# Row tables laid out ahead of the first layer's loop, their padding rows cleared by ScalarE's queue in and behind that loop

## What is computed

```
h = jnp.maximum(_layernorm(x, axis=-1), 0.0)
x = x + _L0_gnn_ref(h, L0_gnn_W, L0_gnn_Bv, src, dst, edge_type_6)
h = jnp.maximum(_layernorm(x, axis=-1), 0.0)
x = x + _L1_gnn_ref(h, edge_attr_48, edge_attr_3, ...)      # edge_index = stack([src, dst])
...
    msg = jnp.concatenate([msg_s, msg_v.reshape(E, NV * 3)], axis=-1)
    out = _seg_mean(msg, src, N)          # first half of L1: mean over the edges of each src
...
    node1 = _seg_mean(msg, src, N)        # second half of L1
    return _bn_scalar(node1, bn1_gs, bn1_bs)
```

## Time and profile before

| | |
|---|---|
| median of 3 runs | 23958.75 us (23958.6 to 23959.51) |
| profiled execution, span from first to last instruction | 23994.0 us |
| a time of the profiled execution beside its span | none is given |
| VectorE, GpSimd, TensorE, ScalarE busy | 81%, 67%, 66%, 43% |
| all DMA queues | 1864.35 MB |

### The profile page before, as it was taken

How to read it: one execution, slowest core, us unless ns; L and a number is a source line. 1 busy time by engine, 2 the same in 40 slices (tenths; PEclk the granted TensorE clock), 3 DMA queues, 4 the chain that set the end, 5 groups by cost and what they waited for, 6 DMA issues and landing times.

```text
span 23994.0 us, 483073 instructions
## 1 busy us (share of the span) xinstructions
PE 15946.4 (66%) x137837; PEld 9487.0 (40%) x137837; DVE 19509.6 (81%) x37328; ACT 10304.8 (43%) x23410; POOL 15973.0 (67%) x18227
## 2 busy tenths in 40 slices
PE   5232777777777777766666577766777777777675
PEld 2221333333333333335656333333343333433333
DVE  8114888888888888889999888888888888888888
ACT  1001444444444444449999433333333333333332
POOL 0772777777777777777777566666666666666665
PEclk6555888888888888877777788888888888888887
DMA  4223333333333333324444222121222222222221
GB/s 142 52 50 132 111 111 106 110 111 111 106 109 111 111 107 109 111 97 118 118 118 118 65 40 40 40 40 40 40 40 40 40 40 40 40 40 40 40 40 37
DMA packets 1355296, 1864.35 MB, mean 78 GB/s; under 512 B 497379, under 2 KB 1137507, under 8 KB 1298789
## 3 DMA queue, kind: packets, MB, share of 16 engines
q1 hardware_dynamic: 835620, 1342.87, 18.2%
q0 software_dynamic: 483776, 469.85, 9.2%
q10 hardware_dynamic: 35842, 50.96, 0.6%
HBM read 1452.58 MB, written 409.77 MB: 78 GB/s over the span
## 4 chain that ended last, share of the span: by engine, by line
DVE 42%; issue 23%; POOL 16%; DVEq 6%; DMA 4%; ACT 3%; PE 3%; ACTq 1%; POOLq 1%; SPq 0%
POOL rows_d L731 13%; DVE arena L1767 11%; DVE arena L1716 7%; DVE arena L1774 6%; DVE arena L1758 5%; DMA rows_d<-arena 4%; DVEq L1794 4%; POOL arena L622 3%; DVE arena L1723 3%; ACT arena L1204 2%; DVE arena L1789 2%; DVE arena L1649 1%; DVE arena L1748 1%; DVE arena L1751 1%; PE wide L978 1%
## 5 line engine op out<-in xcount | busy, mean ns | idle before, releaser
L622 POOL DMA_INDIRECT arena<-s_tab,arena x7072 | 6703.2, 948 | 3772.1 <-issue 2032.1
L731 POOL DMA_INDIRECT rows_d<-arena x6656 | 6424.9, 965 | 2426.7 <-issue 2309.7
L1053 PE MATMUL wide<-w,arena 64*128 64x320 f32 x14144 | 3202.5, 546 | 2843.6 <-DVE arena L1758 2840.6
L978 PE MATMUL wide<-w,arena 64*128 64x320 f32 x13312 | 2975.3, 536 | 2257.1 <-DVE arena L1640 1639.7
L1649 DVE TENSOR_REDUCE arena<-arena 128x40 f32<-128x640 f32 x3328 | 2693.5, 809 | 428.3 <-DMA rows_d<-arena 427.6
L1640 DVE TENSOR_TENSOR arena<-wide,arena 128x640 f32<-128x640 f32 x3328 | 2653.0, 818 | 235.8 <-PE wide L978 167.0
L1053 PEld LDWEIGHTS wide<-w,arena 64*128 64x128 f32 x14144 | 1265.6, 210 | 3954.1 <-issue 2198.5
L1758 DVE TENSOR_TENSOR arena<-wide,arena 128x640 f32<-128x640 f32 x3536 | 2807.3, 815 | 0.2 <-PE wide L1053 0.2
L1767 DVE TENSOR_REDUCE arena<-arena 128x32 f32<-128x640 f32 x3536 | 2780.7, 806 | 0.0
L978 PEld LDWEIGHTS wide<-w,arena 64*128 64x128 f32 x13312 | 1189.1, 209 | 3150.7 <-issue 1778.3
L1039 PEld LDWEIGHTS duo<-ident_sb,arena 128*64 128x64 f32 x14144 | 1623.4, 175 | 1107.9 <-issue 1107.9
(11 more groups left out here) (208 smaller groups left out, 26899.6 us busy)
## 6 DMA issues: line engine op xcount, KB each, us to landing
arena<-rows_d SPq DMA_DIRECT2D x3536, 172.0 KB, 2.3
arena<-in_attr SPq DMA_DIRECT2D x208, 1024.0 KB
arena<-rel SPq DMA_DIRECT2D x208, 1024.0 KB
arena<-in_attr_rows SPq DMA_DIRECT2D x208, 768.0 KB
arena<-s_tab,arena POOLq DMA_INDIRECT x7072
rows_d<-arena POOLq DMA_INDIRECT x6656
rows_d<-zero ACTq DMA_DIRECT2D x198, 172.0 KB, 1.8
side<-arena SPq DMA_DIRECT2D x16, 1040.0 KB
```

Source lines behind the costliest of these rows:

```text
L622: pool.indirect_dma_start(out=dst_, out_offset=None, in_=tab, in_offset=bass.IndirectOffsetOnAxis(ap=idx, axis=0)).then_inc(signal, 16)
L731: pool.indirect_dma_start(out=rows_d[t // 4], out_offset=bass.IndirectOffsetOnAxis(ap=ui[:, s % GPT, t:t + 1], axis=0), in_=M[:, s % GPT, ...
L978: last = pe.matmul(wide[k % 2][:, j, 0:WN], hT[half, s % 2, k * P:(k + 1) * P], w2_sb[0][half, :], start=True, stop=True)
L1053: last = pe.matmul(wide[k % 2][:, j, 0:WN], bhT[half, s % 2, k * P:(k + 1) * P], w2_sb[1][half, :], start=True, stop=True)
```

## The change

The layout (stage 3) is moved ahead of the first layer's loop on VectorE, and its product ahead of that loop on TensorE. On ScalarE the stores of the bin numbers move ahead of the loop too, behind a wait for the layout (`laid_out`). The clears move into the loop: a turn copies out four groups, and behind each group's copy the two half groups of one bin are cleared, for `cleared` turns; later turns run without. The bins that are left and the two closing half groups are cleared behind the loop, and the square root comes behind those.

```diff
--- before.py
+++ after.py
@@ tensor
+            pe.wait_ge(spread_done, 1)
+            half = TPG * HB // 2
+            for i in range(2):
+                pe.matmul(wide[0][:, i, 0:half], ones[0:TPG * LO, :], spread[0:TPG * LO, i * half:(i + 1) * half],
+                          start=True, stop=True).then_inc(count_done, 1)
+
             pe.wait_ge(R.set_up, 1)
...
-            pe.wait_ge(spread_done, 1)
-            half = TPG * HB // 2
...
@@ scalar
             act.wait_ge(bound_out, 1)
-            turns = act.value_load(last_turn_sb[0:1, 0:1], min_val=2, max_val=TURNS - 1) + 1
+            last_turn = act.value_load(last_turn_sb[0:1, 0:1], min_val=2, max_val=TURNS - 1)
             R = R0
+            act.wait_ge(laid_out, 1)
+            act.dma_start(bin_d.rearrange("(h p j) -> p h j", h=2, j=8), gbin).then_inc(bin_out, 16)
+            act.wait_ge(bin_out, 16)
+            act.dma_start(bin_sb[:, :], bin_d.unsqueeze(0)).then_inc(bin_out, 16)
...
+            def clear_bin(b):
+                for h in range(2):
+                    clear_rows(h, act.value_load(zrow[0:1, h, bass.ds(b, 1)], min_val=0, max_val=DUMP * HALF))
+
+            clearing = act.alloc_register("clearing")
+            act.reg_mov(clearing, last_turn)
+            act.reg_alu(clearing, clearing, NB // GPT, ALU.min)
+            cleared = act.snap(clearing, min_val=2, max_val=NB // GPT)
...
                     last.then_inc(R.out_ready, 1)
+                    if clears:
+                        clear_bin(g)
...
             with act.Else():
-                with act.Fori(0, turns) as it:
-                    out_copies(it, False)
-            root(small[:, 1, :], 2, sqrt_out)
...
-            with act.Fori(0, NB) as b:
-                for h in range(2):
-                    clear_rows(h, act.value_load(zrow[0:1, h, bass.ds(b, 1)], min_val=0, max_val=DUMP * HALF))
+                with act.Fori(0, cleared) as it:
+                    out_copies(it, False, True)
+                with act.Fori(cleared, last_turn + 1) as it:
+                    out_copies(it, False, False)
+            with act.Fori(cleared * GPT, NB) as b:
+                clear_bin(b)
             for h in range(2):
                 clear_rows(h, act.value_load(zrow[0:1, h, HB:HB + 1], min_val=0, max_val=(NG + NB) * HALF))
+            root(small[:, 1, :], 2, sqrt_out)
...
@@ vector
             dve.sem_inc(R.x_free, GPT)
             dve.sem_inc(R.inputs_free, GPT)
-            turns = dve.value_load(last_turn_sb[0:1, 0:1], min_val=2, max_val=TURNS - 1) + 1
...
             dve.wait_ge(hot_used, PIECES)
             HT = TPG * LO
             link(tt(spread[0:HT, 0:HT], banks[3][0:HT, 0:HT], tmask[0:HT, :], ALU.mult))
...
             dve.sem_inc(laid_out, 1)
+            turns = dve.value_load(last_turn_sb[0:1, 0:1], min_val=2, max_val=TURNS - 1) + 1
...
```

More of the change, by code:

```diff
@@ L927, in _ @@
                     sum0_window(it)
-            pe.wait_ge(spread_done, 1)
-            half = TPG * HB // 2
-            for i in range(2):
-                pe.matmul(wide[0][:, i, 0:half], ones[0:TPG * LO, :], spread[0:TPG * LO, i * half:(i + 1) * half],
-                          start=True, stop=True).then_inc(count_done, 1)
             def edges():
@@ L1164, in out_copies @@
                     last.then_inc(R.out_ready, 1)
+                    if clears:
+                        clear_bin(g)
             act.wait_ge(R.set_up, 1)
             with act.If(act.value_load(any_wide[0:1, 0:1], min_val=0, max_val=1) > 0):
-                with act.Fori(0, turns) as it:
-                    out_copies(it, True)
+                with act.Fori(0, cleared) as it:
+                    out_copies(it, True, True)
+                with act.Fori(cleared, last_turn + 1) as it:
+                    out_copies(it, True, False)
             with act.Else():
-                with act.Fori(0, turns) as it:
-                    out_copies(it, False)
-            root(small[:, 1, :], 2, sqrt_out)
[L1175 to L1182, removed]
-            with act.Fori(0, NB) as b:
-                for h in range(2):
-                    clear_rows(h, act.value_load(zrow[0:1, h, bass.ds(b, 1)], min_val=0, max_val=DUMP * HALF))
+                with act.Fori(0, cleared) as it:
+                    out_copies(it, False, True)
+                with act.Fori(cleared, last_turn + 1) as it:
+                    out_copies(it, False, False)
+            with act.Fori(cleared * GPT, NB) as b:
+                clear_bin(b)
             for h in range(2):
                 clear_rows(h, act.value_load(zrow[0:1, h, HB:HB + 1], min_val=0, max_val=(NG + NB) * HALF))
+            root(small[:, 1, :], 2, sqrt_out)
             def edges():
@@ L1519, in _ @@
             dve.sem_inc(R.inputs_free, GPT)
+            dve.wait_ge(hot_used, PIECES)
+            HT = TPG * LO
+            link(tt(spread[0:HT, 0:HT], banks[3][0:HT, 0:HT], tmask[0:HT, :], ALU.mult))
+            link(red(gbin_f[0:HT, 0:LO], spread[0:HT, 0:HT].rearrange("p (t l) -> p l t", l=LO), AX, ALU.add))
+            link(tt(spread[0:HT, :].rearrange("p (w l) -> p w l", l=LO), ident_sb[0:HT, 0:HT].unsqueeze(2).broadcast_to([HT, HT, LO]),
+                    gbin_f[0:HT, 0:LO].unsqueeze(1).broadcast_to([HT, HT, LO]), ALU.mult))
@@ new lines, in _ @@
+            dve.sem_inc(spread_done, 1)
+            dve.wait_ge(count_done, 2)
+            for i in range(2):
+                link(dve.tensor_copy(cnt8[:, 4 * i:4 * i + 4, :], wide[0][:, i, 0:4 * HB].rearrange("p (t b) -> p t b", t=4)))
+            for h in range(2):
+                link(red(tot[:, h, :], cnt8[:, 4 * h:4 * h + 4, :].rearrange("p t b -> p b t"), AX, ALU.add))
+            link(ts(need, tot, float(HALF - 1), 1.0 / HALF, ALU.add, ALU.mult))
+            link(ts(need, need, -(0.5 - 0.5 / HALF), MAGIC, ALU.add, ALU.add))
@@ new lines, in _ @@
+            link(ts(need, need, -MAGIC, None, ALU.add))
+            link(dve.tensor_copy(incl[:, 0], need))
+            here, step_ = 0, 1
+            while step_ < HB:
+                link(dve.tensor_copy(incl[:, 1 - here, :, 0:step_], incl[:, here, :, 0:step_]))
+                link(tt(incl[:, 1 - here, :, step_:HB], incl[:, here, :, step_:HB], incl[:, here, :, 0:HB - step_], ALU.add))
+                here, step_ = 1 - here, 2 * step_
+            after = incl[:, here]
+            link(tt(begin, after, need, ALU.subtract))
@@ new lines, in _ @@
+            link(ts(run0, begin[:, :, 0:NB], float(HALF), -FAR, ALU.mult, ALU.add))
+            link(ts(need, need, 0.0, None, ALU.is_gt))
+            link(ts(tot, after, -float(DUMP + 1), None, ALU.add))
+            link(tt(tot, tot, need, ALU.mult))
+            link(ts(zrow[:, :, 0:HB], tot, float(DUMP), float(HALF), ALU.add, ALU.mult))
+            link(ts(zrow[:, :, HB:HB + 1], after[:, :, HB - 1:HB], float(HALF), None, ALU.mult))
+            link(dve.tensor_copy(sum_turns[:, 1:3], after[:, :, HB - 1]))
@@ new lines, in _ @@
+            link(tt(tot[:, 0, 0:1], after[:, 0, HB - 1:HB], after[:, 1, HB - 1:HB], ALU.max))
+            link(ts(tot[:, 0, 0:1], tot[:, 0, 0:1], 1.0 / GPT, -1.0 - 1.0 / GPT - (0.5 - 0.5 / GPT), ALU.mult, ALU.add))
+            link(ts(sum_turns[:, 0:1], tot[:, 0, 0:1], MAGIC, -MAGIC, ALU.add, ALU.add))
+            for h in range(2):
+                link(tt(older, begin[:, h, :].unsqueeze(1).broadcast_to([P, 8, HB]), gno.unsqueeze(2).broadcast_to([P, 8, HB]), ALU.is_le))
+                link(red(tot[:, 1, 0:8], older, AX, ALU.add))
+                link(ts(gbin[:, h, :], tot[:, 1, 0:8], -1.0, float(NB - 1), ALU.add, ALU.min))
@@ L1520, in _ @@
+            dve.sem_inc(laid_out, 1)
             turns = dve.value_load(last_turn_sb[0:1, 0:1], min_val=2, max_val=TURNS - 1) + 1
@@ L1571, in _ @@
                     layer0_window(it)
[L1574 to L1610, removed]
@@ L1611, in _ @@
-            dve.sem_inc(laid_out, 1)
             dve.wait_ge(y_in, 16 * REPL)
```

5 lines of the change are left out of this document (4 added, 1 removed).

## The result

The changed kernel takes 23730.62 us (median of 4 runs, 23728.25 to 23741.48), the kernel before 23958.67 us: ratio 0.9907, 95% interval 0.9893 to 0.9921. That is 228.05 us less; 223.7 were forecast, and 23735 us.

A forecast was written before the change was run, and what follows sets the result against it. Between the layers ScalarE's clears bound the kernel for 227 us; GpSimd's gathers bound the first layer's loop. Savings of 225.6 and 1.1 less losses of 1.7 and 1.3 gave -223.7 us: 23735 us, range 23728 to 23755.

The forecast's parts named there:

- The clears leave the path: Between the layers, SyncE's first edge load no longer waits for 198 clears, moving from 2243.76 to 2018.2: 225.6 us saved.
- The store of `h_parts`: Ahead of the memset between the layers, this store no longer shares DMA with 0.46 MB of clears: 1.1 us saved.
- The clears in the loop: First layer's loop: two clears and a copy take ScalarE 3.0 of 11.9 us a group, covered by GpSimd: cost 0.
- Six clears beside the partial sums' loads: Behind the loop, about four of six clears share DMA with these loads, 176 KB each at 406 GB/s: 1.7 us lost.
- The layout beside the gathers: Ahead of the loop, some 12 gathers beside VectorE's layout each take 0.11 us longer: 1.3 us lost.
- the 1.7 us of cover: Ahead of the loop, GpSimd's gathers outlast the moved layout's chain (649.5 against first scatter at 651.20) by 1.7 us: cost 0.
- The sum: Whole kernel: -225.6 - 1.1 + 0 + 1.7 + 1.3 = -223.7 us.
- The rival of GpSimd being shut out: During the layout, gathers wait for VectorE's running operation, at most 14.4 us lost: 23748 us at most; chance 0.10.
- Clears that slow GpSimd: In the first layer's loop, clears stand in GpSimd's path, 0.43 us 192 times, up to 83 us: 23741 to 23818; chance 0.06.
- The difference taken over from span to median: Whole kernel: the profiled span's 35.25 us above the median of the runs was taken over unchanged, giving 23735 us.

The follow-up runs named there:

- e3r: Kernel before with ScalarE raising `side_free` to SyncE ahead of its clears instead of behind them, on the second chip: 23946.07 us, ratio 0.9994 against the kernel before.
- e2r: Changed kernel with no clear in the loop, all 198 behind it ahead of ScalarE's root, on the second chip: 23920.99 us, ratio 0.9984 against the kernel before.
- fourfold: Changed kernel with six more DMAs of zeros into spare tables for each bin, four times the clearing traffic: 23736.34 us.
- eightfold: Changed kernel with 14 more DMAs of zeros into spare tables for each bin, eight times the clearing traffic: 23740.05 us.
- e8: Changed kernel with clears in the loop's first 14 turns only, not 24, so 86 clears stand behind the loop: 23771.86 us.
- e6: Changed kernel with the layout cut in two, its first part ahead of VectorE's wait for the first layer's constants: 23732.17 us.
- e1r: Kernel before with only the layout and its product moved ahead of the loop, ScalarE's order unchanged, on the second chip: 23956.69 us, ratio 0.9997.

## Why the prediction was right

By its own steps:

- *The clears leave the path:* 225.6 us forecast, 225.5 measured. `e3r` shows why neither SyncE nor the semaphore alone was the reason.
- *The store of `h_parts`:* 1.1 us forecast. From issue to memset it took 13.14 us in place of 13.69: 0.55.
- *The clears in the loop:* cost 0, and 0 it is, within the 1 us by which the loop differs with them (1222.3 us) and without (`e2r`, 1223.2); the fourfold and eightfold kernels show how far the cover reaches. The place of a clear matters, not its being early: behind the loop they cost 188.82 us of waiting for the root (`e2r`).
- *Six clears beside the partial sums' loads:* 1.7 us forecast, 0.2 measured (33.23 us from issue to VectorE's first add, 33.06 before). What was too high is the price of a clear beside the loads, 0.43 us. From the issue of the loads to VectorE's first add `e8` issued 13 clears, and the loads took only 1.4 us longer than in the changed kernel. ScalarE's issues were held up there, and DMA moved 413 GB/s in place of 402 before. That the six were also issued faster than I had reckoned (6.43 us and not 8.3) changed little: the last two were issued behind the first load, as they would have been at the forecast's pace.
- *The layout beside the gathers:* 1.3 us forecast as longer gathers; it cost nothing in the changed kernel, where the 20 gathers ahead of the scatter took 24.97 us against 25.10 before. The step that failed is the 1.7 us of cover. The layout took 620.31 to 641.29, 20.98 us in place of 19.03. Of the 1.95 us more, 1.43 are its product on TensorE, which took 3.04 us in place of 1.61; the other 0.5 are small operations of VectorE that took longer beside a gather (0.45 us in place of 0.27 for one on 128x200). Before, line 932 had matmuls of 499 ns, now line 922 has 874:

```profile
L922 PE MATMUL wide<-T,ones x4: 874/874/1036, 622.0 to 624.2; 80*128 80x400 f32 x4
```

TensorE had waited 22.4 us ahead of it and its granted clock was 0.50 from 612 to 646 us, the lower level of 1.2 GHz; before, the product followed the loop's last join, in a stretch (1868 to 1880 us) at 0.64. In place of a cover of 1.7 us the scatter waited 1.97 us longer than before. That GpSimd's first gather came 2.06 us earlier gave it back, and the first scatter is at 650.98, 0.22 earlier than before. Of the 2.06, 0.90 are the constants' loads, which differ that much between executions (616.6 to 617.8 us), and 1.15 are the faster landing of the gather indices described under `e6`. So this term came out near nothing by luck: two effects of opposite sign, neither of which I had.

- *The sum:* to SyncE's first edge load the traces give -225.5 (clears) - 0.55 (`h_parts`) + 0.17 (partial sums) - 0.22 (first scatter) - 0.26 (last scatter to SyncE's loads, 4.02 in place of 4.28) - 2.43 (from first to last scatter) = -228.8 us. The last term isn't the change's: 832 gathers 3 ns shorter are 2.5 us, and kernels with the old clears have it in part too (`e1r` 1224.0 us, `e3r` 1223.9). Without it the change is worth 226.4 us, and the medians say 228.05 with 13 us between the runs of the changed kernel.
- *The rival of GpSimd being shut out:* the changed kernel doesn't show it, but the mechanism exists: 0.70 to 0.77 us at a gather or scatter that starts just behind a large `TENSOR_TENSOR` with both inputs in SBUF, and some 0.1 us at most at others in the loop. I had looked for 0.11 us at each gather, and had held against the rival that no gather took over 1.189 us; the scatter of 2.33 us stood in my own rows and I passed over it. That the changed kernel has no such gather is the chance of their phase: five of the six traces on the second chip that have the whole layout ahead of the loop have at least one. "SBUF — State Buffer" of the Trainium skill ("SBUF: two separate sides") says that of the two, the one that starts first keeps the port pair that VectorE and GpSimd share for its whole instruction, and that a VectorE operation with two inputs in SBUF takes part in this only against a GpSimd operation that reads SBUF. The traces agree on the inputs, and on the order where VectorE starts first. They differ in the other order: a `TENSOR_TENSOR` that starts 0.14 us behind a gather keeps its 0.99 us. The section's 3100 ns, beside another operation, are not seen here, and a `TENSOR_REDUCE` beside other gathers (0.94 us) cost nothing.
- *Clears that slow GpSimd:* refuted for the 192 clears, and as a price in proportion to traffic; the loop is 5 us longer at four and at eight times the traffic. "DMA: Bandwidth & Descriptors" of the Trainium skill (Queues, rings and completion order) says that the DMA engines take packets from all queues in turn. No run here shows that or speaks against it, as GpSimd's gaps in the loop are those of issue, whatever the traffic.
- *The difference taken over from span to median:* right, and necessary: the span fell to 23727.0, where the sum gave 23770.3, because the first trace of before was itself long.

## What to carry to other kernels

Work of a queue that nothing waits for until later belongs inside an earlier loop whose bound is another engine: there 192 clears cost nothing that shows, and eight times their traffic 9 us in all, while the same clears behind the loop cost almost all that was to be gained (190 of 228 us), as an instruction that others wait for stood behind them. Ask of such a move what the last instruction on the queue is that someone needs, and whether the count of what is left behind the loop fits ahead of it. And check the cover of what must be moved ahead to make it possible: 18 us more of layout cost 14 us by the times and 19 in the trace.

## What was not expected of the hardware

One chip took 29057 us for a kernel that takes 23959 to 23961 on others, with a granted TensorE clock of 0.70 in place of 0.79, and VectorE's, ScalarE's and GpSimd's instructions of the same length as elsewhere (958 ns for line 731). What held that clock down wasn't tried. And one execution had GpSimd's indirect DMAs 2 to 4 ns longer in the median than every other trace, gathers and edge scatters alike. Over more than 14,000 of them this goes with 37 us of the span: more than any of the small terms argued about here.
